# Main products of a grouped convolution as 64x64 tiles from plain slabs, attention output on 512 columns, and all scores of an image ahead of the next image's convolution

## What is computed

```
# 32 models of 16 input channels, 64 hidden units; x1 = x + w2 relu(w1 perceive(x) + b1) + b2
shifts = [x] + [the 8 neighbours of x, one whole 512-channel copy each]
per_g  = concatenate(shifts, axis=1).reshape(b, 32, 144, h, w)     # model m reads rows 144m..144m+143
hdn    = relu(einsum('bmchw,mdc->bmdhw', per_g, w1) + b1)
x1     = x + einsum('bmdhw,mcd->bmchw', hdn, w2) + b2
# attention over the 1024 pixels, 128 inner channels
theta, phi, g = three 1x1 projections of x1
attn   = softmax(theta phi)                                        # 1024 x 1024
out    = batchnorm(w_w (attn g) + w_b) + x1
```

## Time and profile before

| | us |
|---|---|
| median of the runs | 1550.94 (1550.61 to 1552.87) |
| span of the profiled execution | 1548.7 |
| PE busy, granted clock | 1502.4 (97%), 0.997 |
| DVE, ACT, POOL busy | 893.3, 757.5, 282.4 |
| before the loop (first projection starts) | 60.8 |
| 15 rounds of the loop | 94.4 each, 1416.7 |
| from the last image's first projection to the end | 71.2 |

### The profile page before, as it was taken

The page is one execution under the profiler, slowest core; times in us unless marked ns, Lnnn a source line. Parts: engine busy times, 40 slices in busy tenths (PEclk is TensorE's granted clock), DMA queues, the critical chain, the costliest instruction groups (busy, mean ns, idle before and its releaser), DMA issues.

```text
span 1548.7 us, 25435 instructions
## 1 busy us (share of the span) xinstructions
PE 1502.4 (97%) x9420; PEld 825.6 (53%) x9420; DVE 893.3 (58%) x1191; ACT 757.5 (49%) x1205; POOL 282.4 (18%) x134
## 2 busy tenths in 40 slices
PE   7999999999999999999999999999999999999997
PEld 1454655546555464555546555465544655545466
DVE  1474664847557475573746648466474654747445
ACT  3554554545445554454545545454455544545442
POOL 0040310303113040120402104031030311204011
PEclk9999999999999999999999999999999999999998
DMA  8554755646466464656556566474664646656301
GB/s 232 164 202 142 239 166 183 230 139 230 144 212 230 138 233 148 210 195 184 196 153 227 165 188 217 132 248 150 192 233 144 229 141 211 219 161 218 109 0 55
DMA packets 154015, 279.01 MB, mean 180 GB/s; under 512 B 9488, under 2 KB 113424, under 8 KB 154000
## 3 DMA queue, kind: packets, MB, share of 16 engines
q1 hardware_dynamic: 154000, 278.80, 55.7%
HBM read 174.43 MB, written 104.33 MB: 180 GB/s over the span
## 4 chain that ended last, share of the span: by engine, by line
issue 77%; POOL 14%; PE 7%; DVE 1%; ACT 0%; POOLq 0%; DVEq 0%
POOL probs L1113 14%; PE ps L436 2%; PE ps L452 1%; PE ps L463 1%; PE ps L508 0%; DVE x_lo L934 0%; PE ps L479 0%; PE ps L481 0%; PE ps L480 0%; PE ps L494 0%; PE ps L541 0%; PE ps L555 0%; DVE neg_max L896 0%; PE ps L527 0%; ACT x_hi L750 0%
## 5 line engine op out<-in xcount | busy, mean ns | idle before, releaser
L1113 POOL TENSOR_TENSOR probs<-probs,row_inv 128x1024 f32<-128x1024 f32 x128 | 281.7, 2211 | 1246.5 <-DVE row_inv L902 1246.5
L436 PE MATMUL ps<-windows,w_main 128*64 128x512 f32 x2048 | 479.4, 602 | 9.1 <-DMA windows<-in_x 8.3
L709 ACT ACTIVATE hidden<-ps,columns 128x512 f32<-128x512 f32 x512 | 317.1, 689 | 239.4 <-PE ps L463 128.8
L436 PEld LDWEIGHTS ps<-windows,w_main 128*64 128x64 f32 x2048 | 130.0, 135 | 304.6 <-issue 194.7
L923 DVE TENSOR_TENSOR x_lo<-x_lo,x_hi 128x1024 fp32r<-128x1024 f32 x120 | 192.8, 1632 | 12.5 <-ACT x_hi L742 12.2
L877 DVE SCALAR_TENSOR_TENSOR x<-ps,columns,windows 128x512 f32<-128x512 f32 x128 | 96.0, 750 | 168.9 <-PE ps L463 149.4
L896 DVE TENSOR_REDUCE neg_max<-ps 128x1 f32<-128x1024 f32 x128 | 153.9, 1211 | 68.2 <-PE ps L496 66.0
L735 ACT ACTIVATE probs<-ps,neg_max 128x1024 f32<-128x1024 f32 x128 | 142.5, 1114 | 103.1 <-DVE neg_max L896 103.1
L914 DVE STREAM_TRANSPOSE probs<-probs 128x1024 f32<-128x1024 f32 x120 | 146.6, 1231 | 67.8 <-PE ps L543 56.7
L479 PE MATMUL ps<-x_hi,wp_hi 128*128 128x512 f32 x384 | 153.3, 399 | 0.0
L481 PE MATMUL ps<-x_hi,wp_lo 128*128 128x512 f32 x384 | 149.7, 390 | 0.0
(11 more groups left out here) (69 smaller groups left out, 1625.4 us busy)
## 6 DMA issues: line engine op xcount, KB each, us to landing
windows<-in_x SPq DMA_DIRECT2D x112, 562.0 KB, 7.0
rows_out<-probs SPq DMA_DIRECT2D x120, 512.0 KB, 2.7
x_lo<-rows_out SPq DMA_DIRECT2D x120, 512.0 KB, 4.8
out<-x SPq DMA_DIRECT2D x64, 512.0 KB, 3.5
windows<-in_x SPq DMA_DIRECT2D x64, 281.0 KB, 3.8
...
```

Of the source, the lines that this page charges most:

```text
L436: mm(ps[rows, hidden_bank(s, q), :], w_main[:, p, which, :], shifted(windows[:, w, :], unit // UNITS, half), start=True, stop=False, skip_ ...
L709: activation(hidden[:, s % 2, q, :], ps[:, hidden_bank(s, q), :], ACT.Relu, bias=b1s[:, column:column + 1]).then_inc(hidden_ready, 1)
L1113: nc.gpsimd.tensor_tensor(rows, rows, row_inv[:, e].to_broadcast([P, PIXELS]), ALU.mult).then_inc(normalized, 1)
```

## The change

`windows` becomes four plain slabs of 128 channels, loaded once per image in two parts each (`load_top`, 596 of 1124 padded pixels, and `load_rest`). A model's first 128 rows are cut in two chunks of 64 channels, one on partitions 0 to 63 and one on 64 to 127, and each becomes a product on a 64x64 tile. Per slot these are 16 products in four sets of four (`COUPLES`): pairs 0 and 1, then pairs 2 and 3, and then the same with the other chunk, which waits on `main_begun` until the first set of the couple is complete. Waits ahead of main products are instructions of their own (`await_ahead`). `left` and `dx` are as they were; dx has two banks in turn and four held `hidden` buffers, and is placed in twos.

In the loop all eight rows of scores stand ahead of slot 0 of the next image, with the projection (1, G) between rows 3 and 4, and (1, TH) ahead of row 0. Slots 0 and 1 both use the banks 6, 7, 4, 5 and the others the banks 0 to 3, so slot 1's pair q waits for slot 0's relu q. `attend` and `output` work on halves of 512 columns; the results go into `out_half` and are stored by halves. Rows 4 to 7 are fetched back after attend (0), whose buffers they take. The last image's `attend_turned` stays on 256 columns; its outputs are on 512 and stored by blocks.

```diff
-windows = sb("windows", [P, WINDOWS, PADDED])
+windows = sb("windows", [P, BLOCKS, PADDED])
+def main_chunk(p, which, rows_half):
+    c = first_unit(p, which) // 2
+    return c if c % 2 == rows_half else c + 1
...
-HIDDEN_BANKS, BANK_Y, BANK_DX = 5, 6, 5
-FIRST_SLOT_BANKS = [4, 5, 7, 6]
-def hidden_bank(s, q):
-    return (GROUP_PAIRS * s + q) % HIDDEN_BANKS if s > 0 else FIRST_SLOT_BANKS[q]
+BESIDE_SCORES = [6, 7, 4, 5]
+def hidden_bank(n, s, q):
+    if first_image(n):
+        return FIRST_IMAGE_BANKS[(GROUP_PAIRS * s + q + 2) % 6]
+    return BESIDE_SCORES[q] if s < 2 else q
+def dx_bank(s):
+    return 4 + s % 2
+def z_bank(k):
+    return BANK_Z if k % 2 == 0 else BANK_Y
...
+    def load_image(n):
+        sp.wait_ge(x1_ready, n * SLOTS)
+        for b in range(BLOCKS):
+            load_top(n, b)
+        for b in range(BLOCKS):
+            load_rest(n, b)
...
+        if i == HALF_QBLOCKS:
+            attended = sp.snap(n * 2 + 1)
+            sp.wait_ge(y_summed, attended)
...
-    def hidden_main(n, s, q):
-        half, grp = divmod(place_of(n, s), GROUPS)
-        p = GROUP_PAIRS * grp + q
-        await_bank(n, s, q)
-        for which in (FIRST, SECOND):
-            unit = first_unit(p, which)
-            w = window_of(unit)
-            if half == 0:
-                await_window(n, w, grp, "main", q)
-            rows = slice(HIDDEN * which, HIDDEN * (which + 1))
-            mm(ps[rows, hidden_bank(s, q), :], w_main[:, p, which, :],
-               shifted(windows[:, w, :], unit // UNITS, half), start=True, stop=False, skip_group_check=True)
-    def hidden_left(n, s):
+    def await_ahead(semaphore, value):
+        pe.wait_ge(semaphore, value)
+        pe.sem_inc(main_allowed, 1)
+        elif s == 1:
+            await_ahead(hidden_ready, n * SLOT_PAIRS + q + 1)
+        elif s == 2:
+            await_ahead(exp_done, (n - 1) * QBLOCKS + QBLOCKS - 1 + q // 2)
+        else:
+            await_ahead(hidden_ready, n * SLOT_PAIRS + GROUP_PAIRS * (s - 1) + q + 1)
+    def mains(n, s):
+        half, grp = divmod(s, GROUPS)
+        awaited = set()
+        for step in range(2):
+            for c, couple in enumerate(COUPLES):
+                places = [(q, which, (q + step) % 2) for q in couple for which in (FIRST, SECOND)]
+                for q, which, rows_half in places:
+                    b = main_chunk(GROUP_PAIRS * grp + q, which, rows_half) % CHUNKS // 2
+                    if s % GROUPS == 0 and b not in awaited:
+                        awaited.add(b)
+                        await_ahead(top_loaded[b] if half == 0 else rest_loaded[b], (n + 1) * 16)
+                if step == 0:
+                    for q in couple:
+                        await_bank(n, s, q)
+                else:
+                    await_ahead(main_begun, ((n * SLOTS + s) * len(COUPLES) + c + 1) * COUPLE_MAINS)
+                if first_image(n):
+                    pe.wait_ge(w_main_loaded[grp], 16)
+                for q, which, rows_half in places:
+                    p = GROUP_PAIRS * grp + q
+                    chunk = main_chunk(p, which, rows_half)
+                    rows = slice(CHUNK * rows_half, CHUNK * (rows_half + 1))
+                    product = mm(ps[HIDDEN * which:HIDDEN * (which + 1), hidden_bank(n, s, q), :],
+                                 w_main[rows, p, which, :],
+                                 shifted(windows[rows, chunk % CHUNKS // 2, :], chunk // CHUNKS, half),
+                                 start=(step == 0), stop=False, skip_group_check=True)
+                    if step == 0:
+                        product.then_inc(main_begun, 1)
...
+    def attend(n, h):
+        if h == 0:
+            pe.wait_ge(g_split, n + 1)
+            pe.wait_ge(hidden_ready, (n + 1) * SLOT_PAIRS + GROUP_PAIRS + 1)
+        else:
+            pe.wait_ge(out_added, n * SLOTS + GROUPS)
+        pe.wait_ge(pt_split, n * QBLOCKS + HALF_QBLOCKS * (h + 1))
...
+    def output(n, h, k):
+        if k == 0:
+            if h == 0:
+                pe.wait_ge(hidden_ready, (n + 1) * SLOT_PAIRS + GROUP_PAIRS + 2)
+            pe.wait_ge(y_rounded, n * 2 + h + 1)
+        elif k == 1:
+            pe.wait_ge(y_split, n * 2 + h + 1)
+        else:
+            pe.wait_ge(out_added, n * SLOTS + h * GROUPS + k - 1)
+        bank, c = ps[:, z_bank(k), :], slice(k * P, (k + 1) * P)
+        mm(bank, ww_hi[:, c], y_hi[:, :], start=True, stop=False)
+        mm(bank, ww_lo[:, c], y_hi[:, :], start=False, stop=False)
+        if k == 0:
+            pe.wait_ge(y_split, n * 2 + h + 1)
+        mm(bank, ww_hi[:, c], y_lo[:, :], start=False, stop=True).then_inc(z_summed, 1)
...
     def batch of the tensor engine, one call after the other:
-    project(n, 0, TH); dx(n, 7); project(n, 0, PH); project(n, 1, PH); project(n, 0, G);
-    scores(n, 0); scores(n, 1); project(n, 1, TH); scores(n, 2); project(n, 1, G); scores(n, 3);
-    scores(n, 4); scores(n, 5); mains(n + 1, 0, range(0, 4)); hidden_left(n + 1, 0); scores(n, 6);
-    mains(n + 1, 1, range(0, 1)); scores(n, 7); attend(n, 0); mains(n + 1, 1, range(1, 4));
-    output(n, 0, 0); output(n, 0, 1); hidden_left(n + 1, 1); mains(n + 1, 2, range(0, 4));
-    attend(n, 1); dx(n + 1, 0); hidden_left(n + 1, 2); output(n, 1, 0); output(n, 1, 1);
-    mains(n + 1, 3, range(0, 4)); mains(n + 1, 4, range(0, 1)); hidden_left(n + 1, 3); attend(n, 2);
-    dx(n + 1, 1); output(n, 2, 0); dx(n + 1, 2); mains(n + 1, 4, range(1, 4));
-    mains(n + 1, 5, range(0, 1)); hidden_left(n + 1, 4); output(n, 2, 1); attend(n, 3);
-    mains(n + 1, 5, range(1, 4)); hidden_left(n + 1, 5); output(n, 3, 0); output(n, 3, 1);
-    dx(n + 1, 3); mains(n + 1, 6, range(0, 4)); hidden_left(n + 1, 6); dx(n + 1, 4);
-    mains(n + 1, 7, range(0, 4)); dx(n + 1, 5); hidden_left(n + 1, 7); dx(n + 1, 6)
+    project(n, 0, TH); dx(n, 6); dx(n, 7); project(n, 0, PH); project(n, 0, G); project(n, 1, PH);
+    project(n, 1, TH); scores(n, 0); scores(n, 1); scores(n, 2); scores(n, 3); project(n, 1, G);
+    scores(n, 4); scores(n, 5); scores(n, 6); scores(n, 7); mains(n + 1, 0); left(n + 1, 0);
+    mains(n + 1, 1); left(n + 1, 1); mains(n + 1, 2); left(n + 1, 2); dx(n + 1, 0); dx(n + 1, 1);
+    mains(n + 1, 3); left(n + 1, 3); attend(n, 0); mains(n + 1, 4); output(n, 0, 0); output(n, 0, 1);
+    left(n + 1, 4); output(n, 0, 2); output(n, 0, 3); mains(n + 1, 5); left(n + 1, 5); dx(n + 1, 2);
+    dx(n + 1, 3); mains(n + 1, 6); attend(n, 1); left(n + 1, 6); output(n, 1, 0); output(n, 1, 1);
+    dx(n + 1, 4); dx(n + 1, 5); output(n, 1, 2); output(n, 1, 3); mains(n + 1, 7); left(n + 1, 7);
+    pe.wait_ge(out_added, n * SLOTS + SLOTS)
...
     def batch of the scalar engine, from exp_row(n, 4) on:
+    exp_row(n, 4); exp_row(n, 5); relus(n + 1, 0); exp_row(n, 6); exp_row(n, 7); round_row(n, 0);
+    round_row(n, 1); relus(n + 1, 1); round_row(n, 2); relus(n + 1, 2); round_row(n, 3); round_g(n);
+    relus(n + 1, 3); round_y(n, 0); relus(n + 1, 4); round_row(n, 4); round_row(n, 5);
+    round_row(n, 6); relus(n + 1, 5); round_row(n, 7); round_y(n, 1); round_x1(n + 1, 0);
+    round_x1(n + 1, 1); round_x1(n + 1, 2); round_x1(n + 1, 3); relus(n + 1, 6); relus(n + 1, 7);
+    round_x1(n + 1, 4); round_x1(n + 1, 5)
...
     def batch of the vector engine, from transpose_g(n) on:
+    transpose_g(n); find_max(n, 7); invert_sum(n, 4); transpose_row(n, 4); split_row(n, 0);
+    split_row(n, 1); split_row(n, 2); invert_sum(n, 5); invert_sum(n, 6); invert_sum(n, 7);
+    split_row(n, 3); split_g(n); transpose_row(n, 5); transpose_row(n, 6); transpose_row(n, 7);
+    split_y(n, 0); for k in range(BLOCKS): add_out(n, 0, k); split_row(n, 4); sum_x1(n + 1, 0);
+    sum_x1(n + 1, 1); split_row(n, 5); split_row(n, 6); split_row(n, 7); split_y(n, 1);
+    sum_x1(n + 1, 2); sum_x1(n + 1, 3); for k in range(BLOCKS): add_out(n, 1, k); sum_x1(n + 1, 4);
+    for s in range(GROUPS): split_x1(n + 1, s); sum_x1(n + 1, 5); split_x1(n + 1, 4);
+    split_x1(n + 1, 5); dve.wait_ge(stored, (n + 1) * 32)
```

More of the change, by code:

```diff
@@ L450, in hidden_left @@
                     for which in (FIRST, SECOND):
-                        unit = left[q][which]
-                        last = mm(ps[HIDDEN * which:HIDDEN * (which + 1), hidden_bank(s, q), :],
+                        unit = left_unit(GROUP_PAIRS * grp + q, which)
+                        last = mm(ps[HIDDEN * which:HIDDEN * (which + 1), hidden_bank(n, s, q), :],
                                   w_left[rows, grp, which, :],
-                                  shifted(windows[rows, plain_of(unit), :], unit // UNITS, half), start=False,
+                                  shifted(windows[rows, unit % UNITS // 4, :], unit // UNITS, half), start=False,
                                   stop=True, skip_group_check=True)
@@ L826, in _ @@
             nc.scalar.preload_act_table(ACT.Exp)
-            relus(0, 0, range(GROUP_PAIRS))
-            for s in range(1, SLOTS):
-                relus(0, s, range(GROUP_PAIRS))
```

(17 more changed lines are left out.)

905 lines of the change are left out of this document (388 added, 517 removed).

## The result

The changed kernel takes 1579.16 us (median of four runs), the kernel before 1551.79 beside it: 1.017 times as long, interval 1.015 to 1.018. The span is 1577.6. Its parts, as before: 60.6 before the loop (60.8), fifteen rounds of 96.95 (94.42 in the earlier trace rows), and 62.4 for the last image (71.3 in the earlier trace rows). So a round became 2.5 longer, 38 us in all, and the last image gave 8.9 back.

The account below looks back on a forecast made before the run. PE, busy 1502.4 of 1548.7 us, bounds the kernel. A round changes by −2.2 + 0.95 + 1.9 + 1.2 = +1.85, fifteen +27.8, the ends −8: 1568.5, with the median 2.2 above the span 1571; range 1546 to 1600.

Parts of the forecast that it names:

- products: PE's products in a round: longer attend and output products, fewer changes of piece, paired dx, main products unchanged: −2.2 us.
- scores: Score rows 2 and 6 wait for exponentials 0 and 4, 2.8 us a round against 1.85 before: +0.95.
- slots 1 and 5 behind relus: Slot 1, in slot 0's banks, waits 1.75 us for its relus; slot 5 waits 0.15: +1.9 a round.
- attend 0: PE waits 1.6 us for g's subtraction on DVE, delayed by POOL's rows, against 0.38 before: +1.2 a round.
- start: Before the loop: less to load gains 6.1 at most, relu waits take 4.2 back; −3 us, between −6 and 0.
- last image: Outputs on 512 columns and stores by blocks save some of 13 us idle: −5 us, from −12 to +2.
- the rivals of exposed loads and of issue: Main products: weight loads exposed at each set, +34 us, 1605, 15%; or issue cost, +0.3 a slot, 1610, 4%.
- the walk: Timeline ahead of attend 0: POOL rows delay DVE, g's subtraction ends at 9.15 after slot 2's 32-row products begin, PE arrives 7.5.
- The rivals in which POOL doesn't meet g: Ahead of attend 0: POOL's three rows end before g is rounded, no wait, 1.58 a round saved; 1545, 13%.
- The walk without the lock: Ahead of attend 0: without DVE and POOL excluding each other, both subtractions end at 7.35, no wait, sum 24 us lower.

Follow-up runs that it names:

- x_attend256: Changed kernel with attend back on 256-column products in place of 512, nothing else moved: 1583.98 us, a round of 97.30.
- x_scores: Changed kernel with projections (1, TH), (0, G), (1, G) ahead of score rows 2, 4 and 6, in place of one ahead of row 4: 1613.99 us.
- x_banks: Changed kernel with slot 1 in banks 0 to 3, slot 2 in 6, 7, 4, 5, exponentials 6, 7 before slot 0's relus, dx 0, 1 after slot 3's main: 1551.64 us.
- x_inverses: Changed kernel with the inverses of rows 6 and 7 moved behind g's subtraction on DVE: 1554.28 us, a round of 95.31.
- x_best2: Kernel reordered against all three waits, plus roundings of rows 0, 1 each before exponentials 6, 7 and seven hidden-sum banks in first image: 1482.7 us, 0.956 of kernel before.

## Why the prediction held

Forecast 1571 (+20), measured 1579 (+27), in the direction and for the reasons given. By its own steps, per round:

| step | predicted | measured |
|---|---|---|
| products | −2.2 | −2.0 |
| scores (1.46 and 1.54 against 1.85) | +0.95 | +1.15 |
| slots 1 and 5 behind relus (1.87, 0.20) | +1.9 | +2.07 |
| attend 0 (1.68 against 0.31) | +1.2 | +1.35 |
| round | +1.85 | +2.53 |
| start | −3 | −0.2 |
| last image | −5 | −8.9 |

Products is what the other measured rows leave. Every term has its sign and nearly its size; four small errors of one sign make 0.7 a round, 10 us. The ends together came 1.1 better than forecast, and that is luck: the start was 2.8 worse and the last image 3.9 better.

- Products: the mis-sized term is the long product. I took 0.2275 from a run of scores; attend's 24 products take 5.74 to the next piece, 0.23 each with 0.2 for the change. x_attend256 measures attend's part at 0.35 a round where the same prices gave 0.6. Main products at 3.60 a slot, unchanged, held (3.59), and with them the count of four passes for four tiles at once; the rivals of exposed loads and of issue fell. (Their sums were a little off: 128 slots at 0.28 are 36 and not 34, and 64 records at 0.06 are 3.84 and not 3.9, so 1602 and not 1610. That changes no step.)
- Scores: the reload (0.1, not 0.07) and the exponential that ended 0.1 later; the mechanism is as told, and x_scores, with its other costs, has no score row that waits for an exponential.
- Slot 1: 1.87 against 1.75; x_banks takes 1.83 of it away.
- Attend 0: the walk gave g's subtraction an end at 9.15 after the start of slot 2's 32-row products; it is 795.70 − 786.72 = 8.98. The wait is 1.68 for 1.6. Two runs show that POOL makes it. The rivals in which POOL doesn't meet g fell, and x_inverses shows what they would have given. (The walk without the lock said 7.35, which starts the pair where POOL's second row ends, at 5.0; from row 3's rounding at 4.6 it is 6.95. Both are ahead of 7.5.)
- Start: slot 0's 32-row products begin at 15.5, after 18.8 before: 3.4 gained and not 6.1. The prediction gives no working for its 6.1; with a slot's usual 3.59 of main products they would have begun at 9.33 + 3.59 = 12.92, 5.9 earlier than before. What failed is the pace of these first products: they take 15.46 − 9.33 = 6.13, and not for waiting, since PE is busy all through; x_banks, with the same queue there, takes 4.98. Four products run at once, in two records each, and each pass of four has one row of weight loads in the timeline of PEld. These rows are 0.86 apart in slot 0 (11.06 to 11.92) and 0.43 in slot 1 (18.45 to 18.88). The view gives a granted clock of 1.00 for slot 0 (the stretch below), so it doesn't show what halves the pace, and that stays open. The seven slots of the first image lose 0.63 each, as said (0.6). x_best2, with a seventh bank, has a slot of 3.65 there and not 4.22.

```profile
9.33 6.20 PE L400 MATMUL ps<-windows,w_main 64*64 64x512 f32 x32 [9.33 <-DMA w_left<-in_w_lefts]
15.46 1.11 PE L414 MATMUL ps<-windows,w_left 32*64 32x512 f32 x16
```

```profile
11.06 0.27 PEld L400 LDWEIGHTS ps<-windows,w_main 64*64 64x64 f32 x4 [0.58 <-issue]
11.92 0.27 PEld L400 LDWEIGHTS ps<-windows,w_main 64*64 64x64 f32 x4 [0.58 <-issue]
...
18.45 0.18 PEld L400 LDWEIGHTS ps<-windows,w_main 64*64 64x64 f32 x4 [0.25 <-issue]
18.88 0.18 PEld L400 LDWEIGHTS ps<-windows,w_main 64*64 64x64 f32 x4 [0.25 <-issue]
```

```profile
11.30:13.30 2.00, 2.00 (x14) 0.58 (x11) 0.00 (x0) 0.00 (x0) 0.00 (x0) 1.00 1.05 373
```

- Last image: 8.9 and not 5. Before, PE had one wait of 3.17 for a subtraction of DVE and stood at half clock for 6.9 us behind it (0.51, the timeline and the stretch below); after, the longest wait is 0.98 and the clock 1.00. PE is busy 5.78 of the 6.9, and at 0.51 about 2.8 of that (5.78 · 0.49) are the clock's, by estimate; the longest wait gives 2.2 more. I had counted the idle time and not what the clock adds. That the larger outputs gave the rest, some 4, was only argued.

```profile
1508.27 1.09 PE L508 MATMUL ps<-ident,probs 128*128 128x128 f32 x8 [3.17 <-DVE x_lo L934]
```

```profile
1509.50:1516.40 6.90, 5.78 (x19) 4.38 (x18) 3.04 (x5) 4.09 (x6) 2.91 (x2) 0.51 0.01 2
```
